# Second attention on one core: another order for three of VectorE's steps in a turn

## The reference

```python
x = x + 0.5 * _L0_ffn_ref(_layernorm(x), ...)    # top-1 mixture of experts
x = x + _L0_attn_ref(_layernorm(x), ...)         # attention, 8 heads, causal
x = x + 0.5 * _L0_ffn_ref(_layernorm(x), ...)
x = x + 0.5 * _L1_ffn_ref(_layernorm(x), ...)    # top-4 mixture of experts
x = x + _L1_attn_ref(_layernorm(x), ...)         # the second attention
x = x + 0.5 * _L1_ffn_ref(_layernorm(x), ...)
```

```python
q = _rope(x @ Wq, ...); k = _rope(repeat(x @ Wk), ...); v = repeat(x @ Wv)
scores = einsum('bhqd,bhkd->bhqk', q, k) / sqrt(D)
p = softmax(scores, axis=-1)
return einsum('bhqk,bhkd->bhqd', p, v) @ Wo
```

## Time and profile before

| | us |
|---|---|
| median of 3 runs | 1745.87 (1744.73 to 1747.52) |
| the profiled execution, its own time | 1749.62 |
| its span | 1747.7 |
| busy in the span: TensorE (PE) | 1187.7 |
| VectorE (DVE) | 1022.0 |
| GpSimd (POOL) | 790.3 |
| ScalarE (ACT) | 672.2 |

### The profile page before, as it was taken

One profiled execution on the slowest core, in us unless ns is written; L12 is line 12 of the kernel. 1 busy time (PEld: TensorE's weight loads), 2 busy tenths in 40 slices (PEclk: granted clock), 3 DMA queues, 4 the chain that ended last, 5 costly groups with the idle time before them and its releaser, 6 DMA issues.

```text
span 1747.7 us, 31813 instructions
## 1 busy us (share of the span) xinstructions
PE 1187.7 (68%) x10584; PEld 865.1 (50%) x10585; DVE 1022.0 (58%) x2671; ACT 672.2 (38%) x1035; POOL 790.3 (45%) x989
## 2 busy tenths in 40 slices
PE   2198568876199208598976448888885075989772
PEld 2198546654199203497962213444433034979620
DVE  6546656766546884142565757887766941335533
ACT  2154246664044102253531126766672022535310
POOL 0524435553423347666667522222200377666676
PEclk9999689997599559799997758999895587999986
DMA  9233134430133001454641100000000013646422
GB/s 363 65 94 111 38 104 144 151 123 2 36 95 87 25 24 49 130 191 161 192 128 49 42 14 2 2 0 0 0 1 1 24 49 120 198 156 199 145 60 62
DMA packets 100089, 150.10 MB, mean 86 GB/s; under 512 B 21520, under 2 KB 54928, under 8 KB 99216
## 3 DMA queue, kind: packets, MB, share of 16 engines
q1 hardware_dynamic: 58768, 75.30, 13.1%
q0 software_dynamic: 20480, 41.98, 8.1%
q10 hardware_dynamic: 20736, 31.47, 5.4%
HBM read 74.16 MB, written 74.45 MB: 85 GB/s over the span
## 4 chain that ended last, share of the span: by engine, by line
PE 26%; POOL 25%; DVE 16%; issue 14%; DMA 10%; SPq 4%; ACT 3%; DVEq 0%; ACTq 0%; POOLq 0%
POOL slots_top L624 15%; POOL AREA L1098 10%; PE PS L845 5%; DMA slots_top<-XN,ROW 4%; DMA AREA<-results_top,ROW 4%; SPq L1346 3%; PE PS L298 3%; PE PS L300 2%; PE PS L299 2%; PE PS L1789 2%; DVE AREA L1961 2%; DVE XN L407 2%; PE PS L1776 2%; PE PS L1764 2%; DMA query_rows<-AREA 1%
## 5 line engine op out<-in xcount | busy, mean ns | idle before, releaser
L624 POOL DMA_INDIRECT slots_top<-XN,ROW x320 | 317.4, 992 | 365.3 <-DVE ROW L578 225.0
L1098 POOL DMA_INDIRECT AREA<-results_top,ROW x320 | 304.6, 952 | 243.2 <-issue 87.8
L1009 DVE SCALAR_TENSOR_TENSOR AREA<-PS,AREA 128x512 f32<-128x512 f32 x96 | 66.4, 692 | 233.9 <-ACT AREA L983 209.8
L908 PE MATMUL PS<-WGU,AREA 128*128 x768 | 186.2, 386 | 0.0
L1961 DVE TENSOR_REDUCE AREA<-PS 128x4 f32<-128x1024 f32 x128 | 156.8, 1225 | 38.9 <-PE PS L1764 36.6
L1881 ACT ACTIVATE AREA<-PS,AREA 128x1024 f32<-128x1024 f32 x128 | 142.8, 1116 | 87.2 <-PE PS L1776 85.1
L908 PEld LDWEIGHTS PS<-WGU,AREA 128*128 128x128 f32 x768 | 141.4, 194 | 16.7 <-ACT AREA L972 0.7
L1379 POOL TENSOR_TENSOR AREA<-AREA 128x1536 f16<-128x1536 f32 x32 | 92.9, 2903 | 99.9 <-ACT AREA L1594 99.9
L417 PE MATMUL PS<-IDF,XN 128*128 128x128 f32 x192 | 48.7, 411 | 129.5 <-DVE XN L407 129.5
L930 PEld LDWEIGHTS PS<-WD,AREA 128*128 128x128 f32 x768 | 100.2, 191 | 12.7 <-DVE AREA L1004 8.2
L930 PE MATMUL PS<-WD,AREA 128*128 x768 | 102.0, 276 | 6.3 <-DVE AREA L1004 6.3
(11 more groups left out here) (257 smaller groups left out, 3147.4 us busy)
## 6 DMA issues: line engine op xcount, KB each, us to landing
AREA<-slots_top SPq DMA_DIRECT2D x96, 256.0 KB
results_top<-AREA ACTq DMA_DIRECT2D x96, 256.0 KB
slots_top<-ZERO SPq DMA_DIRECT2D x24, 512.0 KB, 3.1
AREA<-slots_top SPq DMA_DIRECT2D x48, 128.0 KB
results_top<-AREA ACTq DMA_DIRECT2D x48, 128.0 KB
AREA<-query_rows SPq DMA_DIRECT2D x48, 128.0 KB, 2.9
slots_top<-XN,ROW POOLq DMA_INDIRECT x320, 2.2
AREA<-results_top,ROW POOLq DMA_INDIRECT x320, 2.5
```

Of the source, the lines that this page charges most:

```text
L624: nc.gpsimd.indirect_dma_start(out=L.xs[q], out_offset=bass.IndirectOffsetOnAxis(ap=ROW[:, n:n + 1], axis=0), in_=XN[:, t * D:(t + 1) * D] ...
L908: ins = nc.tensor.matmul(o, XTF[:, v, j * P:(j + 1) * P], w, start=True, stop=True)
L1009: nc.vector.scalar_tensor_tensor(out=HF[:, v, :4 * P].rearrange("p (j h) -> p j h", h=P), in0=got, scalar=1.0 / SX, in1=HA[:, :4 * P].rear ...
L1098: nc.gpsimd.indirect_dma_start(out=slots[L.tag][u][:, c * D:(c + 1) * D], out_offset=None, in_=L.ys[g * GT // L.tiles], in_offset=bass.Ind ...
```

## The change

Three of VectorE's steps in a turn stand elsewhere; no instruction is added or removed. The negated maxima of tile c+2 are written in slot 3 of turn c, right behind the fourth maximum, instead of at the head of turn c+1. The norm of tile c-2 stands in slot 1 instead of slot 2, and the output addition of tile c-3 in slot 2 instead of slot 1. The waits of each step go with it, with their counts moved by one tile for the negated maxima.

```diff
--- before.py
+++ after.py
@@ -1950,28 +1950,28 @@
 
             def turn(i, c):
                 t = i * 8 + c
-                if tile_exists(i, c + 1):
-                    wait(dve, b_max, 4 * t + 8)
-                    wait(dve, b_q1tr, t + 2)
-                    nc.vector.tensor_scalar(QP[(c + 1) % 4][:, :, 24], MX[:, (c + 1) % 2, :], -1.0 / MSCALE, None,
-                                            ALU.mult).then_inc(b_m.sem, 1)
                 for g in range(4):
                     if tile_exists(i, c + 2):
                         wait(dve, b_s, 4 * t + g + 9)
                         nc.vector.reduce_max(by_group(MX[:, c % 2, :], g),
                                              PS[:, 2:4, :].rearrange("p b (r k) -> p b r k", k=256), axis=AX.X
                                              ).then_inc(b_max.sem, 1)
+                    if g == 3 and tile_exists(i, c + 2):
+                        wait(dve, b_max, 4 * t + 12)
+                        wait(dve, b_q1tr, t + 3)
+                        nc.vector.tensor_scalar(QP[(c + 2) % 4][:, :, 24], MX[:, c % 2, :], -1.0 / MSCALE, None,
+                                                ALU.mult).then_inc(b_m.sem, 1)
                     if g == 0 and tile_exists(i, c + 1):
                         wait(dve, b_q2tr, t + 2)
                         wait(dve, b_st, 4 * t)
                         nc.vector.tensor_copy(QT2[:, (c + 1) % 2, :], bank1[:, 0:512]).then_inc(b_q2.sem, 1)
-                    if g == 1 and tile_exists(i, c - 3):
+                    if g == 1 and tile_exists(i, c - 2):
+                        norm(i, c - 2)
+                    if g == 2 and tile_exists(i, c - 3):
                         wait(dve, b_y, t - 2)
                         x = X[:, bass.ds((t - 3) * D, D)]
                         nc.vector.scalar_tensor_tensor(out=x, in0=banks(0)[:, 352:480], scalar=1.0 / SX, in1=x,
                                                        op0=ALU.mult, op1=ALU.add).then_inc(b_oadd.sem, 1)
-                    if g == 2 and tile_exists(i, c - 2):
-                        norm(i, c - 2)
                     if g == 3 and not last and tile_exists(i, c - 3):
                         wait(dve, b_oadd, t - 2)
                         statistics(t - 3)
```

## The result

The changed kernel takes 1788.15 us (median of 4 runs, 1780.85 to 1791.21) against 1745.3 us for the kernel before, measured beside it. The estimated ratio is 1.0233, with a 95% interval of 1.0207 to 1.026; the medians lie 43 us apart, which is a ratio of 1.0246 and inside that interval. The forecast of 1767.5 had the direction and the place, and half of the size.

What follows compares the result with a forecast made beforehand. No single engine fills the second attention; a loop of waits between VectorE and TensorE sets the turn. 15 x 0.83 + 9 x 1.04 + 0.8 - 1.0 = +21.7 us on 1745.87 gives 1767.5, range 1760 to 1776 (0.60).

Steps and rivals of the forecast that it cites:

- The place: Output addition in group 2's slot: TensorE's projection waits for the same turn's addition, q_four queued behind, in 24 loop turns.
- rivals 3, 4 and 5: Projection runs on a previous turn's addition, 1748.6 (0.02); early maxima free q_four, 1736 (0.02); gain and loss offset (0.02).
- +0.12 for the maxima's wait: On VectorE, negated maxima wait for the fourth maximum, so group 0's maximum starts 0.12 us later; bounds 0 and 0.20.
- +0.83 for a fast turn: Late addition delays projection and q_four; after 0.31 us of slack, a full-clock turn grows 0.83 us, from 8.23 to 9.05.
- The other bound that I named, 0.14: Handoff from the addition's end to TensorE's projection: 0.05 us taken, 0.14 as other end, from ScalarE's handoff to q_four.
- The count of slow turns held at nine: Nine loop turns before were counted as slowed by falls of the clock, 1.19 us each; the sum kept nine.
- 15 x 0.83 and 9 x 1.04: Loop terms of the sum: 15 fast turns at +0.83 us, nine slower turns at +1.04 us, 12.5 + 9.4.
- Rival 1: TensorE's added pause makes the clock fall in more turns; all 24 slow gives +41.5 us, about 1787; chance 0.22.
- The upper end of the range, 1785: The forecast range, 1760 to 1776, was said to go to just below rival 1's end, given as 1785.
- -0.2 was foretold: Outside the 24 loop turns: +0.8 us for the maxima's wait in about 7 turns, less 1.0 in the last turns.
- the 1.0 us booked for it: In the last turns the norm no longer stands behind the output addition: 0 to -4.3 us possible, -1.0 taken.

Runs made afterwards that it cites:

- late projection: Changed kernel with TensorE's projection of tile c+5 moved from slot 2 to slot 3, behind the scores; ratio 0.999 to the kernel before.
- the two places of the maxima: Kernel before with only the negated maxima moved: right behind the fourth maximum, ratio 1.0076; between statistics and rotation, ratio 1.0023.
- the fastest one: Kernel before with projection in slot 3, turned values and output product in slot 2, norm and output addition in VectorE's slot 2; ratio 0.9939 to before.
- the first filler: Changed kernel with the matmuls of values 2 issued twice more, result unused, in TensorE's pause ahead of the projection; ratio 1.0188 to the kernel before.

## Why the prediction was right and wrong

**The place: right.** The projection waits for the addition of the same turn (b_oadd at c - 2), in all 24 turns of the loop, and q_four behind it. The late projection shows it, and rivals 3, 4 and 5 are out.

**+0.12 for the maxima's wait: right in kind, 0.17 in size.** The wait itself is 0.13 (the two places of the maxima), against the 0.12 from L1934. The rest is spacing that I took from a single row: the instruction behind the negated maxima follows after 0.11, not 0.08. The Trainium skill ("VectorE: DVE Perf Modes", "The DRAIN you can't avoid") measured on chained copies that a semaphore costs nothing extra, and that doesn't carry over to these kernels. The prediction left out that the same section has a next instruction that isn't held start earlier: here L1934 starts 0.23 us behind the start of L1932, which takes 0.31, and there a wait has something to cost.

**+0.83 for a fast turn: measured +0.98.** Group 2's maximum starts 6.12 behind the fourth maximum where 6.06 was worked out. From the addition's end to the projection it is 0.24 to 0.29 us, not 0.05. I had taken the price from q_four behind the negated maxima, whose operands have fixed addresses; the projection's have addresses from registers, and the profile shows a register instruction at its weight load. Whether that is the difference was not tried. The other bound that I named, 0.14, was too low as well. Against it, q_four follows the last product after 0.15 and not 0.24. 24 x 0.15 = 3.6 us of the miss.

**The count of slow turns held at nine: the step that failed.** The terms 15 x 0.83 and 9 x 1.04 let the change leave the falls as they were, nine turns with 0.21 more each, 1.9 us; it was 12.0. The falls went from 9 to 16 and their turns from about 9.5 to about 10.7 us. The price of a fall rose by 0.19, close to the 0.21 of the sum; what it had wrong was the number. That is 10.1 of the 13.7 us by which the loop missed (35.5 against 21.8). Nine was right for the kernel before, though 11.5 us by 1.19 is 9.7: the falls there cost 1.28 on the mean, and 0.55 are the loop's jump. Rival 1 named the mechanism at 0.22, and its time for all 24 turns, 1787, was where the kernel landed, in part by luck: it had 24 slow turns where there are 16, fast turns are longer than it had them, and of the 43 us some 6.5 are not located in the stage at all. The reason that I gave it, the new pause, is refuted: that pause can be filled and the falls stay. They start behind group 0's stretch in every kernel without added transposes. Of that stretch the change moved q_four, and the kernels with the maxima's move alone have 13 to 15 falls, the one with the addition alone has 9. Why early maxima bring falls, and why both moves together bring 16 or 17, stays open. The Trainium skill ("TensorE: Matmul & The Clock Gate", "A second HAM failure mode") tells of a kernel in which frequent short pauses of TensorE make the clock swing between its levels. That fits group 0's stretch, where four transposes a turn left 2 falls of 16, and not the pause ahead of the projection, which was filled and left 15.

**The upper end of the range, 1785**, left rival 1's end out, and it should not have: falls were already there in nine of 24 turns, and nothing in the sum said how a longer turn would change that.

**Outside the loop:** +0.8 in the stage where -0.2 was foretold. The last two turns are as long as before, 7.40 and 7.34, so the norm's place ahead of the addition gave nothing there, against the 1.0 us booked for it.

**Not located** are some 6.5 us between the stage's 36.3 and the medians' 43, in executions without a profile.

## What to carry to other kernels

Before a step is moved on one engine, look up who waits for its semaphore, with the count worked out to the turn: a consumer that shows no wait today may have 0.6 us of slack, and then everything queued behind it on an in-order engine moves too. If the producer must be late, move the waiting instruction behind the work that sets the turn; here that cost nothing. And where the granted clock falls in some turns already, find the stretch in front of the falls and put work there that must be done anyway, before counting microseconds at full clock.

## What the runs showed of the hardware

- Moving the projection into the stretch ahead of the falls took them from 9 (11 in a second profile) to 1 in 24 turns, and 9.8 us off the loop, without shortening one turn at full clock.
- Adding four transposes a turn to TensorE's loop (with eight turns in its body) made one turn in each of the two inner jumps of the loop take 15.6 to 16.6 us. In the longest, 1351.28 to 1367.92, TensorE stands idle for 3.92 us and waits for nothing that the profile shows, the granted clock is at 0.50 for some ten microseconds from within that pause on, and instructions are loaded by DMA:

```profile
1356.15 0.61 PE L1776 MATMUL PS<-AREA 32*128 32x256 f16 x4 [3.92 <-issue]
```

```profile
q8 instruction: 4, 0.07, 2.0%
```

  The page counts 79 such packets in both kernels with these transposes, and 60 in before, after and the fastest one, whose turns at the jump take 8.4 to 11.0 us. No such packet falls into the jumps of before. The loop with 384 matmuls more in all (the first filler) has 72 packets and one turn of 14.4. That the loading is what TensorE stood idle for is a reading of these numbers; no run tested it.
